# A four-kind transformer stack on one core: ternary feed-forward blocks in a new order, the second block's mean and scale made one stage earlier, and the ternary weights made in scattered halves

## The reference

```python
x = x + _L0_attn_a_ref(_layernorm(x), ...)   # twice: retention, then silu feed-forward
x = x + _L0_ffn_ref(_layernorm(x), w_up, w_down)
x = x + _L0_attn_b_ref(_layernorm(x), ...)   # window attention
x = x + _L0_ffn_ref(_layernorm(x), w_up, w_down)

def _ternary_linear(x, w):
    alpha = jnp.mean(jnp.abs(w))
    w_t = jnp.sign(w) * (jnp.abs(w) > 0.5 * alpha)
    rms = jnp.sqrt(jnp.sum(x * x, axis=-1, keepdims=True)) / jnp.sqrt(d)
    return jnp.einsum('bsd,fd->bsf', x / (rms + EPS), w_t)

h = gelu(_ternary_linear(x, w_up)); return _ternary_linear(h, w_down)
```

## Time and profile before

| | us |
|---|---|
| Device time, median of 3 (1664.41 to 1668.26) | 1667.95 |
| The profiled execution, its own time | 1668.09 |
| Its span, first to last instruction | 1666.3 |

### The profile page before, as it was taken

How to read it: one execution, slowest core, us unless ns; L and a number is a source line. 1 busy time by engine, 2 the same in 40 slices (tenths; PEclk the granted TensorE clock), 3 DMA queues, 4 the chain that set the end, 5 groups by cost and what they waited for, 6 DMA issues and landing times. The chain is left out here.

```text
span 1666.3 us, 36165 instructions
## 1 busy us (share of the span) xinstructions
PE 1503.4 (90%) x12802; PEld 1235.2 (74%) x12834; DVE 1029.9 (62%) x2252; ACT 914.8 (55%) x1727; POOL 789.6 (47%) x852
## 2 busy tenths in 40 slices
PE   2999996999989999959999798868999999969887
PEld 2777875899977888748998677756777777747776
DVE  3777774655548778745568465545777777645553
ACT  4565552655536555525554466644666666645665
POOL 1466764211115666643223155546666666524554
PEclk9999997999999999969999899987999999979999
DMA  6000000000010000020000100000000000000001
GB/s 224 2 2 1 0 2 23 10 1 0 1 51 2 2 1 1 2 89 26 14 25 1 35 1 1 0 1 1 2 0 0 0 0 0 1 1 14 26 26 39
DMA packets 21073, 26.17 MB, mean 16 GB/s; under 512 B 1888, under 2 KB 19040, under 8 KB 20832
## 3 DMA queue, kind: packets, MB, share of 16 engines
q1 hardware_dynamic: 18416, 21.64, 3.9%
q10 hardware_dynamic: 2544, 3.04, 0.6%
HBM read 20.48 MB, written 4.19 MB: 15 GB/s over the span
## 5 line engine op out<-in xcount | busy, mean ns | idle before, releaser
L374 DVE TENSOR_TENSOR ffn_h_lo<-ffn_h,ffn_h_hi 128x512 fp32r<-128x512 f32 x128 | 114.3, 894 | 139.9 <-ACT ffn_h_hi L526 139.9
L525 ACT ACTIVATE ffn_h<-ffn_hp,c_b 128x512 f32<-128x512 f32 x128 | 88.3, 690 | 178.8 <-PE ffn_hp L608 178.5
L374 DVE TENSOR_TENSOR ternary_ffn_h_lo<-ternary_ffn_h,ternary_ffn_h_hi 128x512 fp32r<-128x512 f32 x128 | 90.3, 712 | 125.1 <-ACT ternary_ffn_h_hi L526 123.9
L619 PE MATMUL ffn_yp<-down_hi,ffn_h_hi 128*128 128x256 f32 x512 | 146.3, 286 | 0.0
L619 PE MATMUL ffn_yp<-down_lo,ffn_h_hi 128*128 128x256 f32 x512 | 143.0, 279 | 0.0
L619 PE MATMUL ffn_yp<-down_hi,ffn_h_lo 128*128 128x256 f32 x512 | 142.8, 279 | 0.0
L299 POOL TENSOR_TENSOR ternary_ffn_h_sq<-ternary_ffn_h 128x512 f32<-128x512 f32 x64 | 84.0, 1320 | 121.6 <-ACT ternary_ffn_h_hi L526 121.5
L619 PE MATMUL ternary_ffn_yp<-down_ternary,ternary_ffn_h_hi 128*128 128x256 f32 x512 | 132.4, 293 | 0.0
L903 POOL TENSOR_TENSOR ret_qk<-ret_qk,ret_qk_sin 128x512 f32<-128x512 f32 x64 | 82.8, 1293 | 103.4 <-DVE ret_qk_sin L993 102.6
L525 ACT ACTIVATE ternary_ffn_h<-ternary_ffn_hp 128x512 f32<-128x512 f32 x128 | 76.6, 598 | 97.7 <-PE ternary_ffn_hp L608 91.2
L619 PE MATMUL ternary_ffn_yp<-down_ternary,ternary_ffn_h_lo 128*128 128x256 f32 x512 | 127.6, 283 | 0.0
(11 more groups left out here) (246 smaller groups left out, 4657.8 us busy)
## 6 DMA issues: line engine op xcount, KB each, us to landing
X<-in_x SPq DMA_DIRECT2D x8, 512.0 KB, 12.7
staging<-in_w SPq DMA_DIRECT2D x4, 1024.0 KB, 8.0
ffn_x_in<-in_x SPq DMA_DIRECT2D x8, 512.0 KB, 3.8
out<-X SPq DMA_DIRECT2D x8, 512.0 KB, 2.9
rotary<-in_rotary ACTq DMA_DIRECT2D x1, 1024.0 KB, 11.9
staging<-in_w_up SPq DMA_DIRECT2D x1, 1024.0 KB, 4.8
staging<-in_w_down SPq DMA_DIRECT2D x1, 1024.0 KB, 7.5
staging<-in_wqkv ACTq DMA_DIRECT2D x1, 768.0 KB, 8.1
```

What stands on the lines that cost most here:

```text
L374: nc.vector.tensor_tensor(h_lo[:, m % R, :], h[:, m % R, :], h_hi[:, m % R, :].bitcast(F32), ALU.subtract).then_inc(h_ready, 1)
L525: nc.scalar.activation(h[:, m % R, :], hp[m % 2][:, :], fn, bias=bias)
L619: last = nc.tensor.matmul(yp[k][t // 2][:, (t % 2) * D:(t % 2 + 1) * D], x[:, m % R, t * P:(t + 1) * P], w[:, m, :], start=(m == 0 and t % ...
```

## The change

Five things are edited, all in `ffn` but the second.

1. **Order in the ternary stages.** `residual` of a block moves from slice 7 of the next block to slice 0 of the block after that, ahead of `hidden_low`. `normalise` stays at slice 0 but now stands behind `hidden_low`. The transposes move from slices 1 and 4 to 3 and 5, the second half of `square_sums` from 1 to 2, the statistics from slices 2, 3, 4 to 1 and 2. On GpSimd `scales` is cut in two: five instructions (`squared_scales`) behind the square of slice 2, and the last power (`last_scale`) at the head of the next step, past `inverse_rms`. On ScalarE `odd_square` goes behind `inputs`.
2. **Block 1 measured a stage earlier.** mean_var and scale move into buffers that live across stages. Retention 0 and 1 and feed-forward 1 now also take the statistics of block 1 of the next stage and its scale; that stage starts with KNOWN = 2 blocks.
3. **Order in the plain stages.** Block 1 is treated as every other (0, 1, 4), with the statistics at slices 1 and 2, so the scale and `add_constants` behind it on GpSimd come two slices earlier.
4. **Weight total.** The four absolute sums move from step 3 to slices 4 to 7 of step 2, the total to step 3 slices 0 and 2, the limits to slice 4.
5. **Ternary pieces.** Each of the eight is cut into its two instructions, and the sixteen halves are put at three slices of step 3, six of step 8 and seven of step 9, where before two stood in every slice of step 8.

The core of the diff:

```diff
+        MEASURED = TOTAL + (next_norm == "ternary")
+        KNOWN = 2 if ready else 0
+        at_first, at_second = (3, 5) if ternary else (1, 4)
+        pieces_at = {at: k for k, at in enumerate([(3, m) for m in (5, 6, 7)] + [(NB, m) for m in (1, 2, 4, 5, 6, 7)] +
+                                                  [(NB + 1, m) for m in range(1, 8)])}
-            return (2, 3, 6) if isinstance(b, int) and b == 1 else (0, 1, 4)
...
-                pool.sem_inc(scale_done, 1)
+                pool.sem_inc(scale_done, KNOWN)
...
-                    for m in range(MF):
-                        if m % 2 == 0 and live(b, NB):
+                    if unmeasured(g - 1):
+                        last_scale(g - 1, 1 - k)
+                    for m in range(0, MF, 2):
+                        if live(b, NB):
                             even_square(b, m)
-                        if m == 4 and fresh(g):
-                            scales(g, k)
+                        if m == 2 and unmeasured(g):
+                            squared_scales(g, k)
                         if m == 4 and live(b - 1, NB):
                             inverse_rms(b - 1, 1 - k)
...
+                        if m == 0 and ternary and live(b - 2, NB):
+                            residual(b - 2, k)
                         if live(b, NB):
                             hidden_low(b, m)
-                        if m == at_norm and m > 0 and fresh(g - 1):
+                        if m == 0 and ternary and fresh(g - 1):
                             normalise(g - 1, 1 - k)
...
-                        if m == 7 and ternary and live(b - 1, NB):
-                            residual(b - 1, 1 - k)
...
-                if g == 3 and m == 7 and make_ternary:
+                if g == 3 and m == 4 and make_ternary:
                     weight_limits()
-                if g == NB and make_ternary:
-                    ternary_piece(m)
+                if make_ternary and (g, m) in pieces_at:
+                    ternary_piece(pieces_at[g, m])
...
+            def second_scale():
+                kinds = 2 if first is not None else 1
+                pool.wait_ge(mv_done, NB + 2)
+                pool.wait_ge(scale_work, 2 * NB + 1)
+                apart(pool, pool_waited)
+                nc.gpsimd.tensor_scalar(work[:, 0, 0, :], mv[:, 1, :, 1], EPS, None, ALU.add).then_inc(eps_added, 1)
+                pool.wait_ge(eps_added, kinds * (NB + 1) + 1)
+                nc.gpsimd.tensor_tensor(next_scale[:, 1, :], work[:, 0, 0, :], minus_half[:, 0:TB], ALU.pow)
```

More of the change, by code:

```diff
@@ L587, in body @@
                             inputs(g - 1, 1, 1 - k)
+                        if ternary and m % 2 and live(b, NB):
+                            odd_square(b, m)
                         if m == 2 and ternary and live(b - 1, NB):
@@ L676, in body @@
                             up_product(b, m, k)
-                        if ternary and m == 1 and live(b - 1, NB):
+                        if ternary and m == 2 and live(b - 1, NB):
                             square_sums(b - 1, 1)
@@ L962, in statistics @@
                     at_least(dve, mv_done, b)
-                    if first is not None and not last_block(b):
+                    if first is not None and not last_block(b) and not after_last(b):
                         x_wait(b, at)
```

111 lines of the change are left out of this document (60 added, 51 removed).

## The result

The changed kernel took 1619.45 us (median of four runs, 1617.92 to 1623.68); the kernel before took 1667.53 us on the same chip. The ratio is 0.972, with a 95% interval of 0.970 to 0.974. The forecast was 1620.0 us with a range of 1610 to 1636. The profiled execution took 1617.92 us, its span is 1615.9.

The account below looks back on a forecast made before the run. TensorE, busy 90%, was taken as the bound, waiting on the order of others' work and losing clock. 25.7 + 4.3 - 0.2 + 10.4 + 8.9 - 1.0 = 48.1 us off 1668.1 gave 1620.0 us, range 1610 to 1636.

Parts of the forecast that it names:

- Block ends: Ternary stages: the new order removes all TensorE waits for xn and squares at block ends, 25.7 us.
- Start of ternary 0: xn no longer waits for statistics and scales, only for GpSimd's increment behind the loads: 4.3 us gained, 4.0 idle left.
- Start of ternary 1: Nothing known in advance, so the 9.31 us wait stays; block 1's statistics ahead of xt_lo lose 0.2 us.
- Feed-forward stages: Feed-forward 0 and 1: waits for xn (8.2 us) and the weight total (2.2) go, together 10.4 us.
- Tails: Last square_sums of each ternary stage stands behind the last down_product, exposing its copy: 0.5 us lost twice, -1.0.
- One wait stays: Rival, ternary block ends: only squares or only xn come in time, twelve ends keep about 1.05 us: 1636 us, chance 0.15.
- it only moves the waits: Rival, ternary block ends: the waits move elsewhere, 25.7 us and 3.1 of clock not gained: 1649 us, chance 0.05.
- The additions hold h_lo: Rival, plain blocks: GpSimd's earlier additions hold two h_lo, TensorE waits 2.1 us in seven blocks: 1635 us, chance 0.12.
- Slower: Rival, ternary block ends: a late inverse holds residual and the h_lo behind it, stopping TensorE: 1692 us, chance 0.04.
- No change: Rival, whole kernel: time stays the same, within about 0.3% (5 us); chance 0.02.
- the sum has 8.9: Clock term, feed-forward 1 and two block ends: time lost to the lowered clock returns with the waits, 8.9 us (bounds 0 and 8.9).

Follow-up runs that it names:

- gain_late_tail: Changed kernel, but ternary 0 scales declared before GpSimd's wait for loads, and a ternary stage's last square sums back at slice 1: 1614.44 us.
- transposes_back: Changed kernel with only the ternary stages' transposes, copies and low parts of xn back at slices 1 and 4: 1667.25 us.
- total_back: Changed kernel with absolute sums, weight total and the sixteen halves of the pieces back at their old places: 1622.67 us.
- changed_again: The changed kernel itself, unedited, timed again beside later kernels on the same chip: 1620.91 us.
- scales_back: Changed kernel with GpSimd's six scale instructions in one piece ahead of the inverse and the second half of square sums at slice 1: 1621.37 us.
- stats_back: Changed kernel with the plain feed-forward stages' statistics back in slices 2 to 4, scale and additions later with them: 1627.04 us.
- stats_total_back: Changed kernel with plain-stage statistics in slices 2 to 4, and absolute sums, weight total and pieces in their old places: 1627.94 us.
- order_back: Changed kernel with the old order in the ternary blocks; early measurement of block 1 and moves of weight total and pieces kept: 1652.67 us.

## Why the prediction was right, point by point

*Block ends, 25.7 us and 3.1 of clock.* Right in size and in both margins: no wait is left at any block end, and taking the order back cost 33.2 us, 4.2 of them (6.70 instead of 2.89 us, and the clock) expected at the start of ternary 0. The step argued with the margins of two queues, as if each edit served one of them. The runs weigh the edits differently. The late transposes are worth 20.8 us alone and 47.8 if missing from the rest; the rest without them costs 14.6 us. Most of what the square gained came from the earlier aggregate on VectorE, not from the smaller number of instructions ahead of it. The prediction reckons with twelve to fourteen ends; the trace has ten with both waits (ten for h_sq) and one more for block 1's xn in ternary 1.

*Start of ternary 0, 4.3 us.* The mechanism stood as told: GpSimd's increment is held by the loads and xn takes 2.83 us beside two squares. The transposes come 9.4 us into the stage, before 13.8, a gain of 4.4. The idle left was 2.89 us and not 4.0, because more of block 0's work fits ahead of transposes at slice 3. I gave nothing back for the clock there; in this execution it stayed full behind the wait, in another it did not. With half of the 25.7 us the terms for this stage make 12.8 + 4.3 + 1.7 - 0.5 = 18.3; the stage gained 19.1.

*Start of ternary 1, -0.2.* Measured 9.30, 1.50 and 1.41 us, as before: nothing lost. The stage gained 14.6 us against 12.8 + 1.4 - 0.5 - 0.2 = 13.5.

*Feed-forward stages, 10.4 us and 5.8 of clock.* The size was nearly right: 14.7 us in feed-forward 1 against 15.6 of the sum, and block 1 of feed-forward 0 waits no more. In the traces these 14.7 are 10.4 us of waits (4.69, 2.21, 2.88 and one of 0.59 for xt_lo that the sum does not have) and 6.4 of clock loss (8.6 to 2.2), less 2.1 for the longer plain blocks. The step that failed is inside it. I credited 8.2 us (2.2 + 1.5 + 2.9 + 1.6) to the moves of weight total and pieces and priced the earlier statistics at zero. Taken back alone, the moves bring 1.8 us of waits back and the statistics 2.9, both together 4.7, and in none of the three traces did the clock fall behind these waits. The prediction had the fact in its hands (the additions begin two slices earlier) but used it only as a danger, for the h_lo they would hold. Additions did hold h_lo, three in a row for 6.01 us in the changed kernel's feed-forward 1, and TensorE did not wait:

```profile
748.59 6.01 DVE L397 TENSOR_TENSOR ffn_h_lo<-ffn_h,ffn_h_hi 128x512 fp32r<-128x512 f32 x3 [1.38 <-ACT ffn_h_hi L552]
```

That they at the same time got out of the way of block 8's xn I did not see.

*Tails, -1.0.* Measured 0.72 us twice, -1.4. gain_late_tail showed that it need not be paid.

*Rivals.* "One wait stays" and "it only moves the waits" are out for this kernel, and transposes_back shows the second was nearer than a chance of 0.05 suggests: one constant set otherwise gives 1667 us, with every other gain in place. "The additions hold h_lo" is out: the holding is there, the wait is not (total_back alone has one for h_lo, 0.80 us). "Slower" had the inverse late; it was early by more than 3 us. "No change" is out by the interval.

The sum of 48.1 against 48.1 of the medians is better than its parts, and the last decimals are luck. Two things that the sum gets wrong cancel. Over the whole span the clock loss fell by 13.6 us (42.4 to 28.8; changed_again has 30.3) where the sum has 8.9. The plain blocks, each 0.33 us longer, took back 4.6 us (2.5 in feed-forward 0, 2.1 in feed-forward 1), a term that the sum does not have and whose cause no run shows.

## What to carry to other kernels

Ask of each wait when its consumer comes, not only when its producer ends: moving the consumer (the transposes) by two slices was worth 20.8 us alone, and the reordering of the producers without it cost 14.6. When an instruction is moved, follow what it releases on other engines; here four statistics moved by a slice or two brought GpSimd's additions out of the way of the next block's xn, and took 2.5 us off that wait, where the edit made for it took 0.3. And before a difference of 1 or 2 us is given to an edit, compare the clock loss of the stages. A semaphore increment that stands for something known should stand ahead of waits for anything else on its engine.

## What the runs showed of the hardware

Whether the clock falls behind a wait of 2 to 3 us is not decided by the wait's length. At the start of ternary 0, waits of 2.89 us (the changed kernel) and 2.99 (total_back) left it at 1.00, which is 2.4 GHz; waits of 2.97 us, in changed_again with the very same code and in scales_back, brought it to the lower level of 1.2 GHz (0.50 in the rows), and the stage took 1.7 us longer in changed_again; of the waits of 2.05 to 2.51 us at block ends in transposes_back it fell behind every second one. At block 8's xn it fell behind 2.88 us (the kernel before) and not behind 2.40 and 2.65 (stats_back, stats_total_back). In the four executions with 2.89 to 2.99 us at the start of ternary 0 the clock had fallen once already and come back before the wait: 1.9 us ahead of it in the two where it then stayed up, 2.6 us in the two where it fell again. That is four cases and no rule. Waits of 3.6 us and more at that place (3.61, 4.59, 5.22, 6.70, 8.73) were all followed by half clock. A sum can price such a wait only as a range from 0 to about 2 us.

Stages with the same code differ between executions by 1.5 to 2.6 us of some 190 to 360, with no wait to show for it. In FF0, FF1 and the window stage the clock accounts for most of it. It also hid a loss: feed-forward 0 took 190.7 us before and 190.6 in order_back, but with 3.0 us of clock loss before and none in order_back; its settled block takes 23.3 us instead of 22.97.

Two instructions of VectorE with a single tile as input, the compare of a piece and xn, took 2.63 instead of 0.48 and 3.46 instead of 1.37 us beside GpSimd's additions.
